# Second mixture of an audio tower on one core: tokens sorted by expert and handled in blocks of one expert

## What is computed

```python
h = xf @ shared_w1 + shared_b1
t = swiglu5(h, *shared_act)
z = t @ shared_w2 + shared_b2                      # shared expert, every token
gate_probs = softmax(xf @ gate_w + gate_b)         # 16 experts
w, idx = top_k(gate_probs, 2); w = w / sum(w)
cw = sum(one_hot(idx, 16) * w[..., None], axis=1)
he = einsum('nd,edh->enh', xf, expert_w1) + expert_b1[:, None, :]   # 128 -> 2 x 96
te = swiglu5(he, ...)    # clip(g) * sigmoid(clip(g) * alpha) * scale * (clip(u) + shift)
oe = einsum('enh,ehd->end', te, expert_w2) + expert_b2[:, None, :]  # 96 -> 128
y = einsum('ne,end->nd', cw, oe)
out = h_in + y + z
```

## Time and profile before

| | us |
|---|---|
| median of 3 runs (2593.47 to 2597.68) | 2593.97 |
| profiled execution, its own time | 2596.48 |
| its span (first to last instruction) | 2594.3 |
| TensorE matmul busy | 2353.9 (91%) |
| VectorE busy | 1794.1 (69%) |
| ScalarE busy | 1304.9 (50%) |
| GpSimd busy | 904.1 (35%) |
| moved by DMA | 65.89 MB, mean 25 GB/s |
| mean granted clock | 0.967 |

### The profile page before, as it was taken

One profiled execution on the slowest core, in us unless ns is written; L12 is line 12 of the kernel. 1 busy time (PEld: TensorE's weight loads), 2 busy tenths in 40 slices (PEclk: granted clock), 3 DMA queues, 4 the chain that ended last, 5 costly groups with the idle time before them and its releaser, 6 DMA issues. The chain is left out here.

```text
span 2594.3 us, 42124 instructions
## 1 busy us (share of the span) xinstructions
PE 2353.9 (91%) x14776; PEld 1622.1 (63%) x14776; DVE 1794.1 (69%) x3556; ACT 1304.9 (50%) x2104; POOL 904.1 (35%) x708
## 2 busy tenths in 40 slices
PE   5899999979995999999999889999999679999996
PEld 4667876845553666666666567777777455655553
DVE  4433333447775988888888757677776588888985
ACT  2334445335542677676776656555556233433332
POOL 0000000024442878777787700000000144444443
PEclk9999999989996999999999999999999799999998
DMA  7650000000001000000000000000000100000000
GB/s 266 245 207 17 25 25 9 1 18 2 2 2 66 1 1 0 0 0 0 0 0 0 11 9 1 0 0 0 0 0 0 54 1 5 9 9 5 9 5 12
DMA packets 23256, 65.89 MB, mean 25 GB/s; under 512 B 4392, under 2 KB 13429, under 8 KB 20693
## 3 DMA queue, kind: packets, MB, share of 16 engines
q1 hardware_dynamic: 23124, 64.16, 7.2%
HBM read 44.26 MB, written 19.89 MB: 25 GB/s over the span
## 5 line engine op out<-in xcount | busy, mean ns | idle before, releaser
L1247 POOL TENSOR_TENSOR c_both<-c_hid 128x512 f32<-128x512 f32 x384 | 492.1, 1289 | 143.7 <-ACT c_hid L1220 107.3
L1220 ACT ACTIVATE c_hid<-c_scaled,c_b 128x1024 f32<-128x1024 f32 x384 | 437.1, 1150 | 173.3 <-DVE c_scaled L1294 158.8
L1294 DVE TENSOR_TENSOR c_scaled<-c_p_h,c_shares 128x1024 f32<-128x1024 f32 x384 | 454.4, 1215 | 79.4 <-PE c_p_h L1163 77.8
L1168 PE MATMUL c_p_o<-c_both,c_w 128*128 128x512 f32 x768 | 390.8, 591 | 0.0
L1161 PE MATMUL c_p_h<-c_x_hi,c_w_hi 128*128 128x512 f32 x384 | 291.4, 759 | 2.6 <-DVE c_w_lo L1317 2.6
L2140 POOL TENSOR_TENSOR e_act_t<-e_upw,e_swish 128x512 f32<-128x512 f32 (+1 forms) x156 | 199.3, 1278 | 250.3 <-DVE e_upw L2236 170.8
L2089 ACT ACTIVATE e_swish<-e_gate,e_slope_b,e_slope 128x512 f32<-128x512 f32 (+1 forms) x156 | 127.1, 815 | 285.3 <-DVE e_gate L2225 285.0
L619 POOL TENSOR_TENSOR d_ln_rstd<-d_ln_var,d_ln_power 128x2 f32<-128x2 f32 x48 | 33.4, 696 | 527.4 <-DVE d_ln_var L615 527.4
L1168 PEld LDWEIGHTS c_p_o<-c_both,c_w 128*128 128x128 f32 x768 | 144.4, 188 | 35.9 <-issue 2.2
L2004 PE MATMUL e_p_o<-e_act_t,e_w 128*128 128x512 f32 (+1 forms) x312 | 161.9, 602 | 0.0
L235 POOL COPY a_work<-a_vec 128x64 f32<-128x64 f32 x4 | 1.2, 304 | 443.0 <-PE a_p_A L317 257.6
(11 more groups left out here) (301 smaller groups left out, 5161.0 us busy)
## 6 DMA issues: line engine op xcount, KB each, us to landing
band_scratch<-a_work SPq DMA_DIRECT2D x16, 1024.0 KB, 5.5
a_work<-band_scratch SPq DMA_DIRECT2D x16, 1023.5 KB, 7.1
a_raw<-in_Wc SPq DMA_DIRECT2D x16, 512.0 KB, 3.5
a_work<-in_x_tok SPq DMA_DIRECT2D x16, 256.0 KB, 7.4
c_w<-in_fW SPq DMA_DIRECT2D x2, 2048.0 KB, 9.7
a_work<-in_xT SPq DMA_DIRECT2D x16, 250.0 KB, 3.0
out<-e_o_tok SPq DMA_DIRECT2D x32, 64.0 KB
e_w<-in_eW SPq DMA_DIRECT2D x1, 1664.0 KB, 9.7
```

Source lines behind the costliest of these rows:

```text
L1168: nc.tensor.matmul(p_o[s][:, 0:N], w2[:, q, :], both[q % SLOTS][:, :], start=(q == 0), stop=(q == NQ - 1)).then_inc(s_down, 1)
L1220: nc.scalar.activation(hid[q % SLOTS][:, :, :], scaled[q % SLOTS][:, :, :], ACT.Gelu, bias=b1[:, q:q + 1]).then_inc(s_ge, 1)
L1247: nc.gpsimd.tensor_tensor(both[q % SLOTS][:, :], hid[q % SLOTS][:, 0, :], hid[q % SLOTS][:, 1, :], ALU.add).then_inc(s_bo, 1)
L1294: v.tensor_tensor(scaled[q % SLOTS][:, :, :], p_h[q % SLOTS][:, 0:N].unsqueeze(1).to_broadcast([128, 2, N]), shares[s][:, :, :], ALU.mult) ...
```

## The change

`phase_second_mixture` is rewritten, and `phase_retention` gets an addition. Constants: MAXB = 63 blocks (2 x 6144 / 256 + 15), PERE = 24 blocks at most for an expert, NSLOT = 256 x (16 x 24 + 63 + 1) = 114688 slots in DRAM, each a row of ROW = 130 numbers: 128 channels, the router's share, and an id. 

Retention clears the slots. Routing takes the 12 groups in turn: layer norm into rows, router, two best experts, the shared expert (4-byte products without splitting), each token's rank within its two experts (products with a triangular matrix and with ones, plus a running count), and eight indirect DMAs for a group, each scattering 128 rows to slot expert x 6144 + rank. Then a table is computed, which block holds which expert and where. For 63 blocks of 256 slots SyncE reads two numbers of the table into registers and loads the rows and one expert's weights; TensorE turns the rows and computes up and down products; the result, times the share, is scattered by two indirect DMAs to the rows of `again`. Ids of unused slots are out of bounds, so nothing is written for them. At last both rows of each token are loaded and added to what routing kept in `acc`. The diff, cut:

```diff
 # phase_retention: sync, then gpsimd
+            sp.wait_ge(s_blank, 1)
+            chunks = slots.rearrange("(c p r) k -> c p (r k)", p=128, r=16)
+            for c in range(NSLOT // (128 * 16)):
+                sp.dma_start(chunks[c], blank[:, :]).then_inc(s_cleared, 16)
+            sp.wait_ge(s_cleared, 16 * (NSLOT // (128 * 16)))
...
             ln.inverse_root(pool, 1)
+            nc.gpsimd.memset(blank[:, :], 0.0).then_inc(s_blank, 1)
 # phase_second_mixture
+        RL, RA, RB, RY, RX = 4, 3, 2, len(s_back), len(s_sent)      # 6 and 3
...
+            for sent in s_sent:
+                sp.wait_ge(sent, 16 * 2 * GB * (NG // RX))
+            def load_block(k):
+                i = k % RL
+                if k >= RL:
+                    sp.wait_ge(s_by, k - RL + 1)
+                    sp.wait_ge(s_bi, k - RL + 1)
+                expert = sp.value_load(table[k:k + 1, 0:1], min_val=0, max_val=E1 - 1)
+                at = sp.value_load(table[k:k + 1, 1:2], min_val=0, max_val=NSLOT // 256 - 1)
+                sp.dma_start(xb[i][:, :, :].rearrange("p r c -> p (r c)"),
+                             blocks[bass.ds(at, 1), :, :].rearrange("b p c -> (b p) c")).then_inc(s_load[i], 16)
+                sp.dma_start(wb[i][:, :], weights[bass.ds(expert, 1), :, :].rearrange("e p c -> (e p) c"))\
+                    .then_inc(s_load[i], 16)
...
+            def load_y(g):
+                if g >= RF:
+                    sp.wait_ge(s_fin, g - RF + 1)
+                sp.dma_start(yb[g % RF][:, :, :, :],
+                             again[g * 2 * N:(g + 1) * 2 * N, :].rearrange("(p n i) c -> p n i c", p=128, i=2))\
+                    .then_inc(s_yb[g % RF], 16)
...
+                rows = min(WS, S - r * WS)
+                sp.wait_ge(s_fin, g + 1)
...
+                    sp.dma_start(dst.rearrange("n s c -> s n c"), acc[b * WS:b * WS + rows, g, :, :]).then_inc(s_out, 16)
+            for g in range(RF):
+                load_y(g)
             for g in range(NG):
+                store(g)
+                if g + RF < NG:
+                    load_y(g + RF)
 # tensor
             for g in range(NG):
+                route(g)
+                shared_up(g)
+                if g + 1 < NG:
+                    to_rows(g + 1)
+                prefix(g)
+                if g + 1 < NG:
+                    to_columns(g + 1)
...
+                shared_down(g)
...
+            for k in range(MAXB + 2):
+                if k < MAXB:
+                    turn(k)
+                if 1 <= k <= MAXB:
+                    ups(k - 1)
+                if k >= 2:
+                    down(k - 2)
 # scalar
             for g in range(NG):
+                if g + 1 < NG:
+                    normalise(g + 1)          # four activations and a copy of the rows
+                shared_silu(g)
+                if g + 1 < NG:
+                    copy_x(g + 1)
+                keep(g)
+                if g + 2 < NG:
+                    copy_in(g + 2)
+            for k in range(MAXB + 1):
+                if k < MAXB:
+                    block_x(k)
+                if k >= 1:
+                    block_silu(k - 1)
 # gpsimd
+            def send(g):
+                pool.wait_ge(s_pos, g + 1)
...
+                for i in range(2):
+                    for n in range(GB):
+                        nc.gpsimd.indirect_dma_start(
+                            out=slots, out_offset=bass.IndirectOffsetOnAxis(ap=pos[g % RX][:, i * GB + n:i * GB + n + 1], axis=0),
+                            in_=rows_x[g % RX][:, i, n, :], in_offset=None, bounds_check=NSLOT - 1, oob_is_err=False)\
+                            .then_inc(s_sent[g % RX], 16)
+            def send_back(k):
+                pool.wait_ge(s_by, k + 1)
+                pool.wait_ge(s_bi, k + 1)
+                for r in range(2):
+                    nc.gpsimd.indirect_dma_start(
+                        out=again, out_offset=bass.IndirectOffsetOnAxis(ap=bid[k % RY][:, r:r + 1], axis=0),
+                        in_=by[k % RY][:, r, :], in_offset=None, bounds_check=2 * NB * SP - 1, oob_is_err=False)\
+                        .then_inc(s_back[k % RY], 16)
             for g in range(NG):
+                if g + 1 < NG:
+                    inverse_root(g + 1)
+                exp_gap(g)
+                send(g)
+            for k in range(MAXB):
+                send_back(k)
 # vector
             for g in range(NG):
+                best(g)                       # logits, the two largest
+                if g + 1 < NG:
+                    statistics(g + 1)
+                shared_clip(g)
+                chosen(g)                     # eight match_replace pairs, three comparisons
+                if g + 1 < NG:
+                    negative_mean(g + 1)
+                weigh(g)
+                places(g)
...
+                shared_act(g)
...
+            def block_y(k):
+                dve.wait_ge(s_bd, k + 1)
+                v.tensor_tensor(by[k % RY][:, :, :], q_y[k % 2][:, 0:256].rearrange("p (r c) -> p r c", r=2),
+                                xb[k % RL][:, :, 128:129].to_broadcast([128, 2, 128]), ALU.mult).then_inc(s_by, 1)
+            for k in range(MAXB + 2):
+                if 1 <= k <= MAXB:
+                    block_clip(k - 1)
+                    block_ids(k - 1)
+                if k >= 2:
+                    block_y(k - 2)
+                if 1 <= k <= MAXB:
+                    block_act(k - 1)
+            for g in range(NG):
+                dve.wait_ge(s_yb[g % RF], 16 * (g // RF + 1))
+                v.tensor_tensor(acc[:, g, :, :], acc[:, g, :, :], yb[g % RF][:, :, 0, :], ALU.add).then_inc(s_sum, 1)
+                dve.wait_ge(s_sum, g + 1)
+                v.tensor_tensor(acc[:, g, :, :], acc[:, g, :, :], yb[g % RF][:, :, 1, :], ALU.add).then_inc(s_fin, 1)
```

More of the change, by code:

```diff
@@ L1869, in phase_second_mixture @@
-        sel_r = sb("sel_r", [128, NT - 1, 128], F32R)
-        euler = sb("euler", [ROWS, GB])
-        x_hi = [sb(f"x_hi{i}", [128, N], F32R) for i in range(2)]
-        x_lo = [sb(f"x_lo{i}", [128, N], F32R) for i in range(2)]
+        before = sb("before", [128, 128])
+        ones = sb("ones", [128, 128])
+        ids = sb("ids", [ROWS, 2, NG * GB])
+        first = sb("first", [ROWS, E1])
+        number = sb("number", [MAXB, 1 + PERE])
+        euler = sb("euler", [ROWS, GB])
+        power = sb("power", [ROWS, GB])
@@ L1917, in phase_second_mixture @@
+        s_yb = [sem(f"y_in{i}") for i in range(RF)]
+        s_sum, s_fin, s_out = sem("first_sum"), sem("finished"), sem("stored")
+        again = nc.dram_tensor("e_again", (2 * NB * SP, 128), F32, kind="Internal").ap()
+        weights = nc.dram_tensor("e_weights", (E1, 128, WROW), F32, kind="Internal").ap()
+        blocks = slots.rearrange("(b p r) c -> b p (r c)", p=128, r=2)
+        CONST, TABLE = 16 * 10, 9
         block = ctx.enter_context(nc.Block())
@@ new lines, in _, with store @@
+            for k in range(MAXB):
+                load_block(k)
+            for i in range(RY):
+                sp.wait_ge(s_back[i], 16 * 2 * len(range(i, MAXB, RY)))
+            def load_y(g):
[4 more added lines that the diff above has]
+                    .then_inc(s_yb[g % RF], 16)
+            def store(g):
@@ new lines, in down @@
+            def down(k):
+                i = k % RL
+                pe.wait_ge(s_ba, k + 1)
+                if k >= 2:
+                    pe.wait_ge(s_by, k - 1)
+                for r in range(2):
+                    last = nc.tensor.matmul(q_y[k % 2][:, r * 128:(r + 1) * 128], bact[k % RA][:, r * 128:(r + 1) * 128],
+                                            wb[i][0:HIDR, DN:PR], start=True, stop=True, skip_group_check=True)
+                last.then_inc(s_bd, 1)
+            to_rows(0)
@@ new lines, in _ @@
+            dve.wait_ge(s_more, 1)
+            v.tensor_reduce(which[:, :], passed[:, :], AX.X, ALU.add)
+            v.tensor_tensor(held[:, :], passed[:, :], ends, ALU.mult).then_inc(s_more, 1)
+            dve.wait_ge(s_more, 2)
+            v.tensor_reduce(starts[:, :], held[:, :], AX.X, ALU.max)
+            v.scalar_tensor_tensor(place[:, 1:2], which[:, :], float(PERE), number[:, 0:1], ALU.mult, ALU.add)
+            v.tensor_scalar(place[:, 0:1], which[:, :], float(E1 - 1), None, ALU.min).then_inc(s_more, 1)
```

741 lines of the change are left out of this document (379 added, 362 removed).

## The result

The changed kernel takes 2625.3 us (median of 4 runs, 2621.6 to 2628.1) where the kernel before takes 2593.8 beside it: a ratio of 1.0117, with a 95% interval of 1.0098 to 1.0136. It is slower by 31.5 us. The forecast was 2616, slower by 22. The profiled execution took 2628.1 us with a span of 2626.3, against the 2619 of the sum. Rows from the traces of the changed kernels name lines of their own files.

The account below looks back on a forecast made before the run. The old stage (534.7 us) was taken as bound by TensorE and VectorE together; new terms 27 + 181 + 7 + 270 + 72 = 557 us, 22 more, gave a median of 2616 us, range 2535 to 2715.

Parts of the forecast that it names:

- Start, 27 us: Start of the new stage: loop begins at about 13.6 us, then a cold first turn of 13.4 us.
- Routing, 181 us: Eleven further routing turns, chained through TensorE, VectorE and ScalarE, at 16.5 us each, with ends 14.2 and 18.8.
- GpSimd's circle 8x + 4.1 with x = 1.3: Routing: eight scatters of x us each, plus powers, share and places; 14.5 us, hidden behind the 16.5 us turn.
- The point x = 1.55: Routing: price of one indirect DMA from which GpSimd's circle is no longer covered by the 16.5 us turn.
- From the last turn to the last row, 7 us: After routing: last places some 6 us before the turn's end, then eight scatters 10.4 and a landing of 2.6.
- Blocks, 16 + 62 x 4.1 = 270 us: The 63 blocks: ring of four buffers bounds the period at (3.0 + 5.25) / 2 = 4.1 us, ends 3.0 and 5.7.
- Tail, 72 us: End of stage: first loads 5, groups 0 to 7 18, sixteen 31-row stores 46.6, last landing 2.5 us.
- Retention, nothing: Clearing the slots writes 59.6 MB in retention, hidden under its 272 us loop, so costed at nothing.
- 3.7 as the period under which it would be wrong: Blocks: sign that the prediction is wrong, a block taking under 3.7 us.
- The register load: Blocks: SyncE's register loads taken as 0.9 us each; a 600 ns floor would make the sum 19 us less.
- The rule on GpSimd and VectorE: GpSimd can't write descriptors during VectorE's two-port SBUF instructions; would price the GpSimd-bound rival (2662 us, chance 0.14) or more.
- the faster rival: Routing and blocks: short load circle and high clock, 3.5 us a block, 14.2 a turn; 2554 us, chance 0.36.

Follow-up runs that it names:

- e10: Changed kernel with only TensorE's routing order rearranged, a separate bank for the running count and three hg buffers: 2590.6 us, ratio 0.9983 to the kernel before.
- e2: Changed kernel with eight buffers instead of four for a block's rows and weights: 2545.8 us, ratio 0.9799 to the kernel before.
- e3: Changed kernel without the second of the two indirect DMAs that scatter a block's results back: 2612.3 us, 13 less.
- e4: Changed kernel without a block's two register loads, SyncE loading from fixed addresses: 2562.7 us, 63 less.
- e12: Changed kernel with eight block buffers, split stores and the new routing order, minus the final semaphore clearing: 2515.1 us, against 2482.7 with the clearing.

## Why the prediction was right

The forecast's sign and size held (2616, measured 2625.3), inside its own band of 2589 to 2650, and no rival came about. But the sum of 557 against 568.5 is one of errors that partly cancel: the blocks came out 19 us shorter than forecast, the other four terms 30 us longer. That the size is so near is in part luck. By its steps:

- **Start, 27 us.** 27.9. The loop begins at 2071.13, 13.3 us after the stage, where I had 13.6.
- **Routing, 181 us.** 195.8, the term that was most too low. The turn is 17.0 to 17.3 us at a mean clock of 0.70 and 19.7 at 0.59, where I had 14.2 at the high clock and 18.8 at the low one and took 16.5. The chain was right up to chosen. The step that failed is the one behind it: I let the turn close over ScalarE's Silu and had forgotten that the places wait for the rank products and the running count, 16 short records (the count's eight among them are four products of 4-byte numbers), 3.6 us from 2207.10 to 2210.7. They are in the quoted order of TensorE. e10 puts the count, shared_down and shared_up behind the products that VectorE needs first, all in one edit, and wins 24 to 35 us.
- **GpSimd's circle 8x + 4.1 with x = 1.3.** 1.27 to 1.28 a scatter, and 14.8 us for the circle once it is the bound, where I had 14.5. The point x = 1.55 wasn't reached. Its start 0.8 us behind the places was missing in 4.1; VectorE's part was 1.6 us instead of 2.0.
- **From the last turn to the last row, 7 us.** 11.6. I had the last places 6 us before the end of the last turn; they are ready 0.7 us before it (2280.7 of 2281.4), because VectorE's list has places directly ahead of the activation product and the last turn is itself 3 us shorter. This step was wrong. The scatters (2281.52 to 2291.5) took 10.0 for my 10.4, and their landing 1.5 for my 2.6.
- **Blocks, 16 + 62 x 4.1 = 270 us.** 17.0 + 62 x 3.78 = 251.3. The circle is the one that I described: eight buffers free it (e2), half of GpSimd's work is nothing to it (e3), and without register loads it is shorter (e4). One pass of it in the changed kernel:

```profile
2403.66 0.42 DVE L2471 TENSOR_TENSOR e_by<-e_p_l,e_xb 128x256 f32<-128x256 f32 x1
2403.96 0.44 PE L2102 MATMUL e_p_x<-identity,e_xb 128*128 128x128 f32 x2 [0.47 <-DMA e_wb<-e_weights]
...
2405.40 0.33 SPq L1997 DMA_DIRECT2D e_xb<-slots  x1
2405.92 0.33 SPq L1999 DMA_DIRECT2D e_wb<-e_weights  x1
...
2408.29 0.44 PE L2102 MATMUL e_p_t<-identity,e_xb 128*128 128x128 f32 x2 [2.58 <-DMA e_wb<-e_weights]
```

  From the end of the output product (2404.08) to the turn with the landed block (2408.29) it is 4.2 us: 1.3 for the register loads behind the wait, 0.5 between the issues, 2.4 for the landing. I had 1.8, 0.45 and 3.0. The landing was mis-sized: the nearest row carried 250 KB, these carry 130 and 164. TensorE's and VectorE's part is 3.2 on average, 2.7 where the granted clock is high (1.00 from 2360 to 2380) and 3.8 where it is low (0.60 from 2340 to 2360), for my 3.0. The 4.2 of this pass are 4.5 on average. (3.2 + 4.5) / 2 = 3.85, measured 3.78 with the first four loads, which wait for nobody. The prediction named 3.7 as the period under which it would be wrong; it was near.
- **Tail, 72 us.** 82.0. The sixteen stores took 44.75 us where I had 46.6, the groups before them 19.7 and the start 5.2. Two pieces were mis-sized: the wait for the last landing is 6.0 us, not 2.5, and behind it stands the stage's last line, which the cut diff doesn't show (it is the one that e12 takes out): the clearing of 76 semaphores by GpSimd, which the old stage did not have and which I had passed over: 6.2 us from 2620.1 to the end.
- **Retention, nothing.** Right. From 545 to 700 us the DMA engines moved 387 GB/s at a share of 0.93, the next stage's first load is issued at 815.9 us (815.0 before), and 6.3 MB more in e3 and e4 moved nothing either.
- **The register load.** The Trainium skill's floor of about 600 ns ("DMA: Bandwidth & Descriptors", latency and other measured facts) stood beside my 0.9. In the trace the first two begin at 2293.0 and 2293.8 and the issue follows at 2294.5, 0.75 each with their range checks, and in the pass above both take 1.3. So the trace lies nearer to the figure of the Trainium skill than to mine, and my row, a transfer of 4 KB, was too far off.
- **The rule on GpSimd and VectorE.** The rule of the Trainium skill ("SBUF — State Buffer", the note on VectorE blocking DMAs of GpSimd) would have made x longer beside VectorE's work. For most scatters it did not: of the 126 in the blocks half took 973 ns or less, and the 23 that began under a clip out of PSUM took 975 at most. Those over 1.1 us began while VectorE worked on two operands in SBUF, and ended 0.85 to 1.06 us behind that instruction; in the twelve traces of the changed kernel and its variants this holds for 82 of 83. They are 1122 and 1258 ns under a block's activation product, 1.41 us in e10, where the first scatter of nearly every turn begins under the shared one, and the longest in the first turn:

```profile
2082.68 2.28 DVE L2411 TENSOR_TENSOR e_blob<-e_blob,e_prm 96x2048 f32<-96x2048 f32 x1
2083.75 2.27 POOL L2250 DMA_INDIRECT slots<-e_rows_x,e_pos  x1 [6.61 <-DVE e_pos L2349]
```

  That agrees with the rule in kind, though not every such meeting costs time (in e2 some scatters under the activation product took 0.97 us), and no run moved one of the two away. In e10 it is worth 0.4 us a turn.

The chances: 0.57 for slower was fair, but the faster rival (2554) was further off than its 0.36 says. It needed short turns, short loads and a high clock together; it got the loads in part and none of the others.

## What to carry to other kernels

Leaving work out moves the bound: when no engine is busy for two thirds of a stage, draw each circle with its buffers, its queue and its fixed prices, and try its one number (here four buffers or eight: 75 us) before judging the idea. When an order is changed so that a wait goes, look which instruction of the same engine waits next and what still stands ahead of it; two half moves gave nothing clear of the spread and the whole one at least 24 us. And read a DMA's slowest dimension: a store of 31 rows cost SyncE 2.80 us and one of 32 rows 0.50, and where the transfers lie bare at the end that is the time of the kernel.

## What was unexpected of the hardware

- An indirect DMA of 128 rows keeps GpSimd for 0.97 us, and the next begins 0.30 us later, whether the rows are 512 or 520 bytes; the first of a series starts 0.8 us after its offsets are written. Begun under a VectorE instruction on two SBUF operands it can take up to 2.27 us, and under one that reads PSUM it did not grow.
- Register instructions of SyncE can take 0.7 us instead of 0.02 to 0.15, over a whole stage, in a program that differs from its quick neighbour only behind the last store. The times of its four runs agree (2513 to 2519), so it belongs to the program, not to one execution. 32 us hang on it here, and the cause is open.
- The granted clock of one and the same routing turn differs from turn to turn and from execution to execution: 17.1 us at a mean of 0.70 (a mixture of 1.2 and 2.4 GHz), 19.7 mostly at 0.59. In the blocks a shorter wait for loads raised it from 0.82 to 0.97, so that taking a wait away gave more than the wait.
